# Layer 0: where VectorE prepares the small constants, and in which bank ring their tiny product lies

## The reference, cut to what matters

```python
xn = _layernorm(x)
q, k, v = xn @ w_q.T, xn @ w_k.T, xn @ w_v.T          # 32 wide
sigma_q, sigma_k = elu_plus_one(q), elu_plus_one(k)
memory_output = sigma_q @ memory / clip(sigma_q @ memory_norm, EPS)
local_output = causal sum over earlier tokens of (sigma_q . sigma_k) v / clip(sum, EPS)
g = sigmoid(gate[0])
s = (g * memory_output + (1 - g) * local_output) @ w_o.T
scores = softmax(xn @ W_gate)                         # the two largest of 7 weigh the expert
f = xn @ W_shared.T + weight * (xn @ W_expert.T) + bias
x = x + s * silu(f)
```

## Time and profile before

| | us |
|---|---|
| median of 3 runs (lowest to highest) | 679.46 (679.04 to 682.68) |
| the profiled execution, its own time | 678.19 |
| span of the profiled execution | 676.3 |
| PE busy | 607.6 (90%) |
| DVE busy | 410.7 (61%) |
| ACT busy | 363.8 (54%) |
| POOL busy | 241.2 (36%) |
| mean granted TensorE clock | 0.984 of full |

### The profile page before, as it was taken

One profiled execution on the slowest core, in us unless ns is written; L12 is line 12 of the kernel. 1 busy time (PEld: TensorE's weight loads), 2 busy tenths in 40 slices (PEclk: granted clock), 3 DMA queues, 4 the chain that ended last, 5 costly groups with the idle time before them and its releaser, 6 DMA issues.

```text
span 676.3 us, 12511 instructions
## 1 busy us (share of the span) xinstructions
PE 607.6 (90%) x4085; PEld 397.9 (59%) x4088; DVE 410.7 (61%) x902; ACT 363.8 (54%) x845; POOL 241.2 (36%) x226
## 2 busy tenths in 40 slices
PE   8999969999968999889888988898988898899896
PEld 3884436987856676566656543454656665645353
DVE  5868734754537447573865587545956676356544
ACT  6356837456643624685677433462577469453342
POOL 2000660173470007574657131221257136433131
PEclk9998989999997999999999999999999999999999
DMA  8910223576662211000000400410000000130120
GB/s 291 370 44 0 92 79 93 172 221 182 184 198 74 89 53 29 16 2 10 21 5 1 127 1 0 112 30 17 1 1 2 1 1 1 38 91 0 57 86 16
DMA packets 36415, 47.54 MB, mean 70 GB/s; under 512 B 4736, under 2 KB 22752, under 8 KB 35840
## 3 DMA queue, kind: packets, MB, share of 16 engines
q1 hardware_dynamic: 33376, 39.53, 19.1%
q0 software_dynamic: 2976, 7.21, 3.4%
HBM read 37.42 MB, written 9.31 MB: 69 GB/s over the span
## 4 chain that ended last, share of the span: by engine, by line
PE 55%; DVE 19%; ACT 10%; issue 8%; POOL 4%; DMA 3%; DVEq 0%; ACTq 0%; POOLq 0%
PE bank L591 51%; ACT arena L1213 8%; DVE arena L2273 2%; DMA arena<-slots_in 2%; DVE arena L2258 2%; DVE arena L2316 2%; POOL arena L2593 1%; DVE arena L2281 1%; DVE arena L2417 1%; DVE arena L2267 1%; PE bank L1079 1%; PE bank L774 1%; DVE bank L2309 1%; POOL arena L2601 1%; POOL slots_in L2501 1%
## 5 line engine op out<-in xcount | busy, mean ns | idle before, releaser
L1213 ACT ACTIVATE arena<-bank 128x512 f32<-128x512 f32 (+8 forms) x220 | 123.7, 565 | 107.7 <-PE bank L591 52.1
L1213 ACT ACTIVATE arena<-bank,arena 128x128 f32<-128x128 f32 (+1 forms) x244 | 87.9, 387 | 116.4 <-PE bank L591 52.9
L591 PE MATMUL bank<-arena,w 128*64 128x128 f32 (+3 forms) x544 | 140.5, 413 | 5.0 <-ACT arena L1213 5.0
L591 PE MATMUL bank<-arena 64*128 64x256 f32 (+8 forms) x832 | 108.8, 328 | 6.0 <-ACT arena L1213 5.9
L591 PE MATMUL bank<-xn_b,w 128*128 128x512 f32 (+1 forms) x192 | 91.5, 598 | 5.4 <-DVE arena L2417 3.8
L591 PE MATMUL bank<-arena,work 128*128 128x128 f32 x624 | 84.5, 283 | 11.4 <-DVE arena L2162 9.2
L591 PEld LDWEIGHTS bank<-arena 64*128 64x128 f32 (+3 forms) x832 | 73.2, 169 | 33.0 <-ACT arena L1213 16.8
L591 PEld LDWEIGHTS bank<-arena,work 128*128 128x128 f32 x624 | 77.9, 196 | 22.1 <-issue 13.1
L591 PEld LDWEIGHTS bank<-arena,w 128*64 128x64 f32 (+1 forms) x544 | 61.7, 162 | 35.8 <-issue 23.0
L591 PEld LDWEIGHTS bank<-xn_b,w 128*128 128x128 f32 (+1 forms) x192 | 34.5, 189 | 44.0 <-issue 26.6
L2501 POOL DMA_INDIRECT slots_in<-arena x32 | 33.2, 1039 | 75.8 <-DVE arena L2068 65.9
(11 more groups left out here) (219 smaller groups left out, 886.2 us busy)
## 6 DMA issues: line engine op xcount, KB each, us to landing
work<-in_ew SPq DMA_DIRECT2D x46, 256.0 KB, 3.3
w<-kept SPq DMA_DIRECT2D x32, 128.0 KB, 3.1
work<-kept SPq DMA_DIRECT2D x32, 128.0 KB, 3.2
slots_in<-work SPq DMA_DIRECT2D x2, 1472.0 KB, 17.0
arena<-in_eb SPq DMA_DIRECT2D x46, 64.0 KB, 3.4
arena<-slots_in SPq DMA_DIRECT2D x10, 256.0 KB, 3.8
slots_out<-arena POOLq DMA_DIRECT2D x10, 256.0 KB, 3.5
w_ew<-in_ew SPq DMA_DIRECT2D x1, 2048.0 KB, 11.0
```

Of the source, the lines that this page charges most:

```text
L591: return nc.tensor.matmul(o, lhsT, rhs, start=start, stop=stop, skip_group_check=True)
L1213: return nc.scalar.activation(o, i, f, bias=bias, scale=scale, **kw)
```

## The change

It moves the constants' fourteen VectorE instructions, unaltered, out of `norm0` into a function `constants0`. VectorE calls it in stage 3 of group (0, 0), so behind stage 2 of all groups and ahead of the first state addition. TensorE issues mb behind stage 1 of all groups instead of ahead of it, and into the slow ring instead of the quick one. ScalarE's wait for "consts" moves from stage 2 to the stage that reads ff.

```diff
--- before.py
+++ after.py
@@ -613,6 +613,8 @@
                     o = fresh("quick", "qk0", g)
                     mm(o[0:2 * DM], W0["wqk"], xg).then_inc(*step("qk0", g))
                     yield
+                    if not n:
+                        mm(fresh("slow", "mb")[:, 0:2], mean[:], w1b[:, 4:6]).then_inc(*step("mb"))
                     o = fresh("quick", "kvg0", g)
                     for c in range(C):
                         i = mm(o[:, c * KVG:(c + 1) * KVG], xg[:, cs(c)], W0["wkvg"])
@@ -1161,8 +1163,6 @@
                     for g in range(G):
                         variance(0, g)
                 pe.wait_ge(ready["first"], 16 * 7)
-                now[1] = 0
-                mm(fresh("quick", "mb")[:, 0:2], mean[:], w1b[:, 4:6]).then_inc(*step("mb"))
                 staggered(layer0, now)
                 pe.wait_ge(ready["one"], 16)
                 now[:] = [1, 0]
@@ -1287,7 +1287,6 @@
                     after()
                     fn(ek[:, n], ek[:, n], ACT.Exp, scale=-1.0).then_inc(*step("ek", g))
                     yield
-                    act.wait_ge(*at_of(0, "consts"))
                     after(("kvg0", g))
                     kv = psum("kvg0", g)[:, 0:C * KVG].rearrange("p (c k) -> p c k", k=KVG)
                     fn(vtok0[:, n, :, 0:DM], kv[:, :, DM:2 * DM], ACT.Copy).then_inc(*step("vtok0", g))
@@ -1299,6 +1298,7 @@
                     fn(gw[:, n * C:(n + 1) * C, 1], gw[:, n * C:(n + 1) * C, 0], ACT.Exp).then_inc(
                         *step("gexp", g))
                     yield
+                    act.wait_ge(*at_of(0, "consts"))
                     after(("ff", 0, g))
                     fn(tz0[:, n], psum("ff", 0, g)[:], ACT.Tanh, scale=0.5, bias=half0[:]).then_inc(*step("tz", 0, g))
                     fn(gz0[:, n], psum("ff", 0, g)[:], ACT.Identity, scale=0.5, bias=half0[:]).then_inc(
@@ -1799,6 +1799,9 @@
                                 *step("xn", 0, g))
                             reached[("xc", 0, g, "read")] = reached[("xn", 0, g)]
                     now[1] = 0
+
+                def constants0():
+
                     k = once_v
                     dve.wait_ge(ready["first"], 16 * 7)
 
@@ -1870,6 +1873,8 @@
                         *step("gdiff", g))
                     yield
 
+                    if not n:
+                        constants0()
                     for c in range(C):
                         k = g * C + c
                         after(("kv0", g), *([("state", g - 1)] if g and not c else []))
```

## The result

| | before | changed |
|---|---|---|
| median of 6 runs, us | 680.47 (679.04 to 682.68) | 687.32 (684.69 to 690.21) |
| profiled execution, us | 678.19 | 690.21 |
| mean granted TensorE clock of it | 0.984 | 0.972 |

The ratio of the changed kernel to the one before is 1.0083, interval 1.0048 to 1.0119. The forecast was 683.2, with a range up to 685.2: the direction held, the size did not. The profiled execution is this time the slowest of its six.

The account below looks back on a forecast made before the run. From 15 to 32 us VectorE's chain sets the pace, TensorE close beside it. New wait +2.2 and clock +1.5 make +3.7 us on the median 679.46: 683.2 us, range 680.4 to 685.2.

Parts of the forecast that it names:

- Part 1: Ahead of stage 1: without the constants, VectorE's first pass and all of stage 2 come 1.24 us earlier.
- Parts 2 and 3: Constants return at 25.79; the fourth y0 waits for mb's bank, TensorE idles 4.0 us, first state addition +2.2 us.
- Part 4: TensorE's clock halves after the idle stretch, slowing the fourth y0 and first kv0: +1.5 us.
- case A: Rival taken as forecast: the clock falls behind the idle stretch, +3.7 us, bounds +2.7 to +5.2; chance 0.62.
- add little: Later kv0 at low clock take 1.0 us a group, near the 0.86 us VectorE needs for a group's additions.
- the upper bound: Clock low for 5.1 us after the restart, y0 and all four kv0 at double length: +5.2 us in all.
- The cover: On TensorE ahead of ff: the last a0 ends at 33.7, before ff can start at 34.5.
- The 0.5 us allowed for the runs: Scatter allowance on top of the upper bound against the median, 684.7, ending the range at 685.2.
- B: At the fourth y0 and first kv0: the clock holds at 1.00, +2.2 us, 681.7 us; chance 0.24.
- C: kv0 need not stay behind y0 on TensorE, so the new wait binds nobody: +0.6 us, 680.1; chance 0.09.
- D: Constants slip into VectorE's idle time, keeping stage 1's 1.24 us: a gain, 678.2 us; chance 0.05.
- The rule of the Trainium skill: On TensorE's clock: a long enough idle gap drops it to half rate; sum +3.7 by it, +2.2 without.

Follow-up runs that it names:

- ring_only: Kernel before with one edit, mb put into the slow ring at its old place: ratio 1.0007, 19.30 us from ScalarE's first pass to ff against 17.68.
- filled_gap: Changed kernel with sixteen matmuls of zeros on TensorE between the last kvg0 and the fourth y0: ratio to before 1.0059.
- changed_again: Changed kernel measured a second time, no edit: ratio to before 1.0054.
- changed_third: Changed kernel measured a third time, no edit, on another chip: ratio to before 1.0034.
- changed_fourth: Changed kernel measured a fourth time, no edit, on the last chip: ratio to before 1.0054.
- shared_bank: Changed kernel with mb written into unused columns of the first group's kvg0 bank, taking no slow-ring bank: ratio to before 1.0025.
- split: Against the kernel before: three constant instructions stay ahead of stage 1, eleven move to the first group's stage 5, mb shares num0's bank: ratio 0.9972.
- half_filled: Changed kernel with seven matmuls of zeros ahead of the fourth y0, executed once: 21.34 us from ScalarE's first pass to ff, against 17.68 before.
- ring_only_look: The kernel of ring_only executed once more, for its profile: 19.31 us from ScalarE's first pass to ff, against 17.68 before.
- base_again: Kernel before measured against itself, no edit: ratio 1.0002.

## Why the prediction was wrong

**Part 1 held.** Stage 2 moved ahead by 1.17 us (kvg0 17.97 - 15.17 = 2.80 us after ScalarE's first pass, before 3.97); 1.24 was forecast. One sentence of it fell, though not in this kernel: that the idle time ahead of the fourth qk0 is worth nothing. ring_only took away the wait alone and lost 1.62 us.

**Parts 2 and 3 held in their mechanism, and were a little short.** Order, wait and releaser were as forecast: idle 3.82 us (4.0), the fourth y0 at 13.09 us after ScalarE's first pass (27.78 - 14.64 = 13.14). Without the clock the loss is +2.57 (filled_gap) where I had +2.2: from the start of y0 to the first state addition it took 30.20 - 28.34 = 1.86 us, not 1.47, because y0 took 1.09 to kv0's start instead of 0.92 and the handover from kv0 to VectorE was counted as 0.05 us.

**Part 4 is the first step that failed, by its size:** +1.5 us for the clock, and it measured 1.8 to 2.5 us (2.29 in the first profile, 4.86 - 2.57). The clock fell in all four profiles, as case A had it. On VectorE's chain the forecast was good: the first state addition is at 31.47 - 15.17 = 16.30 us, before 12.39, so +3.9 us, and +3.7 was forecast. What failed is the sentence that the later kv0 "add little" and the reason for which I left the upper bound. The low clock lasted until 34.2, through all of kv0 and into a0; then TensorE needed the whole a0 before ff, and no idle time was left ahead of ff (37.71 against 35.92 + 0.84 = 36.76, when ysc would have released it). The cover that part 3 had found good for 0.8 us at full clock was gone. That is another 0.95 us, in all +4.86 us; the upper bound of +5.2 stood in the text.

**The 0.5 us allowed for the runs are the second, and they alone put the time outside the range.** With +4.4 to +5.0 us on the median of 679.46 the time would have been 683.8 to 684.5, inside it. The six runs gave +6.85 us on a base that had itself moved to 680.47. Of the 4.1 us between 683.2 and 687.32, then, 1.2 are layer 0's (4.86 against 3.7), 1.0 the base's, and 2.0 what the runs lost beyond the profile's layer 0 (6.85 against 4.86). No profile shows a place for these 2.0 that is the same in all four changed kernels, and the other three comparisons gave +3.5, +1.5 and +3.7 us by their medians. That two of their ratios are 1.0054, just the forecast's 0.54%, is luck: their layer 0 lost 4.5 and 4.4 us and not 3.7.

The kernel before alone spreads over 3.6 us in six runs. The spread goes with the time at half clock: over its runs on the three chips the two correlate by 0.57, 0.69 and 0.90. The low stretches are at one place in one run and elsewhere in the next, as the one in layer 1 above. In the profiled execution three more lie behind 330 us, where the profile of before had none (windows of TensorE alone: length, busy, clock, DMA share, GB/s):

```profile
335.00:338.00 3.00, 3.00 (x17) 0.50 0.08 22
427.00:430.00 3.00, 3.00 (x5) 0.50 0.00 0
550.00:553.00 3.00, 3.00 (x12) 0.50 0.00 0
```

changed_again, changed_third and changed_fourth have other sets of such stretches, so these aren't laid to the change.

**Rivals.** B (the clock holds) is what filled_gap measures, and not what the changed kernel does. C (the wait binds nobody) is refuted by the 3.82 us row and by kv0's start behind y0, at 30.27; its price is near what shared_bank shows, +0.90. D (a gain) fell as argued: VectorE had no idle time at the constants' new place. split shows where there was some.

The rule of the Trainium skill that the forecast leaned on ("TensorE: Matmul & The Clock Gate", section "HAM oscillation — how this bites in real kernels") agrees with 22.0 to 22.7 us unfilled against 20.25 us filled. It speaks of a long gap; here the clock also fell behind 2.31 us (half_filled) and 1.69 us (ring_only, ring_only_look).

## What to carry to other kernels

When a small product gets a bank from a rotating ring, its reader's place decides who waits one turn of the ring later: write down that later owner and all that stands behind it in its queue. An idle stretch that this opens on TensorE may bring its clock down (it did at 1.69, 2.31 and 3.82 us here): price the work behind it at half clock, and then ask again whether the engine that had slack still has it. Small preparations belong where their engine waits anyway, split by when each result is first read, rather than in one block.

## What the runs showed that I had not expected

- A wait can be worth having. One piece of 1.69 us idle, followed by kvg0 and y0 at 18.65, was followed by clock 0.50 in both profiles; the same idle time cut into 1.33 and 0.29 us by one 64x512 product was not (ring_only and ring_only_look against base_again; before has 1.38 and 0.29).
- The clock can fall once TensorE is at work again: in half_filled the idle stretch of 2.31 us ended at 27.70, and the clock was 1.00 until 29 and 0.50 from 29.4; in ring_only it ended at 18.65, and the clock was 0.50 from 19.8.
- Matmuls of zeros kept the clock up: 1.00 over 24.5 to 34.5 us in filled_gap.
- The same kernel spread over 693.0 to 701.8 us in 26 runs on one chip, 692.0 to 702.1 in 29 on the next and 678.2 to 685.3 in 29 on the third. One profiled execution is no median: the layer 0 time repeats to 0.01 us at full clock, the whole time does not to 5.
